# Eight masked identities of 128 rows in place of 16 rows of one, for the matmul that opens a counting block

## The reference, cut to what matters

```python
loop = jnp.arange(n, dtype=edge_index.dtype)
src = jnp.concatenate([edge_index[0], loop])
dst = jnp.concatenate([edge_index[1], loop])
deg = jax.ops.segment_sum(jnp.ones_like(dst, dtype=x.dtype), dst, num_segments=n)
...
msg = h[src] * norm[:, None]
out = jax.ops.segment_sum(msg, dst, num_segments=n)
```

## Time and profile before

| what | value |
|---|---|
| median of 3 executions | 856.17 us (855.83 to 856.72) |
| the profiled execution's span, first to last instruction | 855.8 us |
| TensorE busy (matmuls) | 823.9 us, 96% |
| VectorE busy | 672.8 us, 79% |
| ScalarE busy | 270.3 us, 32% |
| GpSimd busy | 58.5 us, 7% |
| mean granted TensorE clock | 0.997 |

### The profile page before, as it was taken

The page is one execution under the profiler, slowest core; times in us unless marked ns, Lnnn a source line. Parts: engine busy times, 40 slices in busy tenths (PEclk is TensorE's granted clock), DMA queues, the critical chain, the costliest instruction groups (busy, mean ns, idle before and its releaser), DMA issues.

```text
span 855.8 us, 13745 instructions
## 1 busy us (share of the span) xinstructions
PE 823.9 (96%) x5022; PEld 531.2 (62%) x5022; DVE 672.8 (79%) x1181; ACT 270.3 (32%) x510; POOL 58.5 (7%) x77
## 2 busy tenths in 40 slices
PE   5999999999899999999999998999999999999995
PEld 4566665566554444445888887886666666655553
DVE  6998885787675757999988889969973196996686
ACT  3443445300111110104554536644311007770000
POOL 2000002001103000000000000002101000000111
PEclk9999999999999999999999999999999999999998
DMA  8000003123131225217111313123212242212231
GB/s 304 4 2 2 1 2 126 43 68 152 62 155 68 74 74 223 87 70 231 54 48 51 103 32 114 58 81 120 91 62 93 75 154 74 93 56 74 74 111 70
DMA packets 24588, 73.55 MB, mean 86 GB/s; under 512 B 2756, under 2 KB 3756, under 8 KB 24398
## 3 DMA queue, kind: packets, MB, share of 16 engines
q1 hardware_dynamic: 23262, 67.61, 23.0%
q0 software_dynamic: 1264, 5.11, 1.8%
HBM read 52.40 MB, written 20.31 MB: 85 GB/s over the span
## 4 chain that ended last, share of the span: by engine, by line
PE 81%; DVE 10%; issue 3%; DMA 2%; ACT 1%; DVEq 1%; SPq 0%; POOL 0%; POOLq 0%
PE psum L949 18%; PE psum L976 18%; PE psum L1057 11%; PE psum L743 9%; PE psum L864 8%; DVE arena L1449 6%; PE psum L755 6%; PE psum L807 4%; PE psum L800 1%; PE psum L964 1%; PE psum L990 1%; DMA arena<-as_scratch 1%; PE psum L901 1%; PE psum L716 1%; DMA arena<-uv_scratch 1%
## 5 line engine op out<-in xcount | busy, mean ns | idle before, releaser
L976 PE MATMUL psum<-arena 128*128 128x257 f32 x800 | 175.4, 381 | 3.7 <-DVE arena L1593 2.6
L1064 ACT ACTIVATE arena<-psum 128x160 f16<-128x160 f32 (+6 forms) x188 | 93.4, 527 | 257.4 <-PE psum L743 74.7
L976 PEld LDWEIGHTS psum<-arena 128*128 128x128 f32 x800 | 151.2, 190 | 27.4 <-ACT arena L1064 2.7
L743 PE MATMUL psum<-arena 128*128 128x512 f16 x720 | 159.4, 379 | 2.4 <-DVE arena L1421 2.1
L949 PE MATMUL psum<-arena 128*128 128x512 f16 x960 | 158.5, 326 | 0.2 <-ACT arena L1064 0.2
L949 PEld LDWEIGHTS psum<-arena 128*128 128x128 f16 x960 | 93.5, 97 | 62.3 <-ACT arena L1064 0.5
L743 PEld LDWEIGHTS psum<-arena 128*128 128x128 f16 x720 | 69.2, 98 | 86.5 <-issue 7.1
L1057 PE MATMUL psum<-arena 128*128 128x512 f16 (+2 forms) x600 | 98.4, 325 | 0.0
L1449 DVE CUSTOM_DVE_ANT_0 arena<-arena 128x1280 bf16<-128x1280 bf16 x50 | 71.0, 1488 | 15.4 <-DMA arena<-as_scratch 9.6
L1057 PEld LDWEIGHTS psum<-arena 128*128 128x128 f16 x600 | 58.3, 97 | 39.8
L1167 ACT ACTIVATE arena<-arena 128x640 f32<-128x640 f32 x80 | 64.6, 836 | 51.5 <-DVE arena L1578 51.3
(11 more groups left out here) (169 smaller groups left out, 710.2 us busy)
## 6 DMA issues: line engine op xcount, KB each, us to landing
arena<-in_L_gnn_W_dram SPq DMA_DIRECT2D x22, 384.0 KB, 3.4
r_scratch<-arena SPq DMA_DIRECT2D x10, 512.0 KB, 2.6
arena<-uv_scratch SPq DMA_DIRECT2D x16, 320.0 KB, 4.4
arena<-r_scratch SPq DMA_DIRECT2D x10, 512.0 KB, 3.8
x_scratch<-arena SPq DMA_DIRECT2D x10, 384.0 KB, 4.5
arena<-x_scratch SPq DMA_DIRECT2D x10, 384.0 KB, 3.5
r_scratch<-arena SPq DMA_DIRECT2D x10, 384.0 KB, 2.6
arena<-r_scratch SPq DMA_DIRECT2D x10, 384.0 KB, 3.9
```

Of the source, the lines that this page charges most:

```text
L743: ins = pe.matmul(o[:, a:b], part[:, k, ds(t * P, P)], w[:, k, a:b], start=(not begun and k == 0 and n == 0 and m == 0), stop=(k == kn - 1 ...
L976: last = pe.matmul(p_att[:, ATT_BANKS[ch][j], 0:HID + 1], pf[n % PSLOTS][:, j * P:(j + 1) * P], xl[ch % H][:, k, 0:HID + 1], start=(k == 0 ...
L1064: act.activation(out_, in_, ACT.Copy, scale=scale).then_inc(signal, 1)
```

## The change

The opening matmul of a block reads all 128 partitions of both operands in place of the first 16. For that, GpSimd makes `own_rows`, eight matrices of 128 x 128 side by side: number j is the identity with all but its rows 16 j to 16 j + 15 zero. The moving operand is a window of `ident_w`, which is widened from 304 to 416 columns. The product is the same 128 x 160 block as before. `ident_w` and `own_rows` move to bytes 185 K and 183 K of each partition, memory that is used for something else later, so `ident_h` gets a tile of its own. TensorE waits once, ahead of block 0, for four new GpSimd instructions (semaphore `own_ok`).

```diff
-        SELF = (T - 1) * WD
-        ident_w = small([SELF + T * WD], f16)
-        ident_h = ident_w[:, SELF:SELF + P]
-        assert SELF >= P - WD and T * WD >= P
+        ident_h = small([P], f16)
...
+        SELF, STEP = (T - 1) * WD, P + WD
+        own_rows = at(183 * KB, [SUBS * P], f16)
+        ident_w = at(185 * KB, [SELF + P - WD + T * WD], f16)
+        assert 4 * D * (T - 1) == 27 * KB and SUBS * P + SELF + P - WD + T * WD <= 2 * D
...
-            for m, shift, width in ((ident, 0, P), (ident_w, SELF, SELF + T * WD)):
+            for m, shift, width in ((ident, 0, P), (ident_w, SELF, SELF + P - WD + T * WD)):
                 pool.affine_select(out=m, in_=m, compare_op=ALU.not_equal, fill=1.0, base=shift,
                                    pattern=[[-1, width]], channel_multiplier=1).then_inc(S["ident_ok"], 1)
             pool.wait_ge(S["ident_ok"], 4)
-            pool.tensor_scalar(less_h, ident_h, -1.0, None, ALU.mult).then_inc(S["iotas"], 1)
+            pool.tensor_scalar(less_h, ident_w[:, SELF:SELF + P], -1.0, None, ALU.mult).then_inc(S["iotas"], 1)
...
             pool.memset(half, -0.5).then_inc(S["half_ok"], 1)
+            pool.memset(own_rows, 0.0).then_inc(S["own_ok"], 1)
+            pool.tensor_copy(ident_h, ident_w[:, SELF:SELF + P]).then_inc(S["own_ok"], 1)
+            pool.wait_ge(S["own_ok"], 2)
+            pool.tensor_copy(own_rows[:, 0:(SUBS - 1) * STEP].rearrange("p (j c) -> p j c", j=SUBS - 1)[:, :, 0:WD],
+                             ident_h[:, 0:P - WD].rearrange("p (j c) -> p j c", j=SUBS - 1)).then_inc(S["own_ok"], 1)
+            pool.tensor_copy(own_rows[:, (SUBS - 1) * STEP:], ident_h[:, P - WD:]).then_inc(S["own_ok"], 1)
...
                 t, row = b // SUBS, b % SUBS * WD
-                own = pe.matmul(o, ident_w[0:WD, SELF - row:SELF - row + P], ident_w[0:WD, SELF - t * WD:SELF - t * WD + T * WD],
-                                start=True, stop=True)
+                own = pe.matmul(o, own_rows[:, b % SUBS * P:(b % SUBS + 1) * P],
+                                ident_w[:, SELF + row - t * WD:SELF + row - t * WD + T * WD], start=True, stop=True)
...
             pe.wait_ge(S["ranges_i"], 1)
             pe.wait_ge(S["iotas"], IOTAS)
+            pe.wait_ge(S["own_ok"], 4)
```

## The result

| | before | after |
|---|---|---|
| median of 4 executions each | 856.11 us (855.83 to 856.72) | 846.2 us (844.18 to 846.28) |
| ratio | | 0.9872 (0.9861 to 0.9884) |
| span of the profiled execution | 855.8 us | 842.3 us |
| time of that execution | (not on record) | 844.18 us |
| last opening matmul starts | 138.8 us | 127.7 us |

The account below looks back on a forecast made before the run. VectorE was taken to set the pace up to 38.8 us, TensorE from there to 138.8. Terms 12.9 - 0.2 + 0.1 - 0.3 gave 12.5 us, so span 843.3 and time 843.7 us; range 842.0 to 847.5, its own narrower one 842.5 to 845.5.

Parts of the forecast that it names:

- The price of an opening matmul: Counting stage, blocks 14 to 79: about 0.10 us lost on each side, 0.195 us gained per block, 12.9 us in all.
- Whenever the number of rows changes: Claimed cause of the gaps around opening matmuls: TensorE's array empties at any change of row count, 0.10 us either side.
- The half-gain rival: Only the side behind the opening matmul gains, its load waiting for blk_free: 6.6 us, 849.6 us; chance 0.07.
- The blocks behind the degrees: Eight counting-stage blocks following one-column matmuls: side ahead gives 0.07 us, not 0.10, so 0.2 us less in all.
- Block 19: Counting stage: TensorE would be ready at 46.31 us but the block's keys come at 46.64, so 0.3 us less gain.
- VectorE becomes the bound: Rival: in the counting stage VectorE can't follow TensorE; loss of 1 to 5 us, 845 to 849 us; chance 0.08.
- 12.9 - 0.2 - 0.3: Counting-stage terms: 66 blocks' gain of 12.9 us, less 0.2 for blocks behind the degrees and 0.3 for block 19.
- GpSimd's setup: Before block 0: four added instructions end at 10.7 us, 14.3 at double price, some 8 us of cover; no cost.
- The forecast's own sign of being wrong: At block 0, listed among what the profile would show if wrong: TensorE's first opening matmul later than 18.6 us.
- The wider mask: Setup: identity mask of 416 columns for 304 lengthens two instructions by 0.13 us each; taken as nothing, at most 0.3.
- Span and time: End of the sum: span 843.3 us turned into time 843.7, as the runs' median was 0.4 above the profiled span.
- All after 140 us shifts with TensorE: Everything behind the counting stage follows no other clock and shifts with TensorE, by one amount.

Follow-up runs that it names:

- e3: Changed kernel with the opening matmul reading 16 to 128 rows, stepped by block of a tile; 850.64 us, one execution, against 855.82 for the kernel before.
- e4: e2 with the 20 bias matmuls of the second layer's residual also reading 128 rows, zeros below row 2; 844.27 us.
- e2: Changed kernel with the four table instructions on ScalarE in place of GpSimd; 843.95 us, and 844.4 us when run again.
- e5: Changed kernel with the four table instructions still on GpSimd but waiting until VectorE's seven int16 passes are done; 844.79 us.
- a1_after_again: The changed kernel run again unaltered; 846.12 us against 857.15 for the kernel before on that chip, ratio 0.9869.

## Why the prediction was right or wrong

- **The price of an opening matmul** was right: 0.17 became 0.07 and 1.07 became 0.97, and by exact starts most blocks gain 0.20 to 0.21. The cause was right in kind: e3 and e4 show that it is the count of rows, not the code around it. "Whenever the number of rows changes" was too wide: 80, 96 and 112 rows lose nothing beside 128. The half-gain rival (the load with its wait isn't pulled ahead) falls: that load starts 0.07 ahead.
- **The blocks behind the degrees** were mis-sized: 0.165 each in my sum, 0.12 measured, since the side ahead gave 0.05 for 0.07 and the side behind 0.07 for 0.10. Eight of them, one of which gained only 0.03: 0.4 us. Blocks 25 and 41, which come right behind such a block with no product between, were counted at 0.195 and gained nothing (L807 of block 25 waits until 56.04 us; what for, the trace doesn't say): 0.4 more. The other blocks' 0.01 above the price gives that back.
- **Block 19** cost 0.26 for 0.3. The rest of the rival "VectorE becomes the bound" did not come: from block 13's first loop matmul to block 79's opening matmul there were 138.83 - 38.96 = 99.87 us by the trace of before, and are 127.7 - 39.90 = 87.8: 12.1 gained, and 12.4 by my terms (12.9 - 0.2 - 0.3).
- **GpSimd's setup was the step that failed.** I costed it at nothing because own_ok had 8 us of cover, and it had: the four instructions ended at 8.9 us, where 10.7 was forecast. I asked only who waits for their end, and not whom their running holds up. VectorE's first L1291 was held for 1.1 us, on the very chain that I had named as setting the pace up to block 13. Measured: block 13 0.94 us late, and 0.9 to 1.0 us given back at block 79 by e2 and e5. The forecast's own sign of being wrong, a first opening matmul later than 18.6 us, came with it (19.2).
- **The wider mask**, taken at nothing, cost some 0.1 us in all the new kernels: its memset lasts 0.43 us for 0.34, VectorE's passes start at 6.74 for 6.61, and with ScalarE's tables block 13 starts at 38.97, where 38.86 was forecast. No run left the wider mask out, so this cause is argued from the times and not shown.
- **Span and time.** The step from 843.3 of span to 843.7 of time was wrong: time is span + 1.8 to 2.2. And the execution profiled before was one in which the VectorE chain set the start of the attention layer, 2.3 us later than TensorE's would have. With both put right, and 11.1 us of gain: 855.8 - 11.1 + 1.8 to 2.2 = 846.5 to 846.9 when that chain is as late as it was, and 2.3 us less, 844.2 to 844.6, when TensorE's comes last. The measured 844.18 to 846.4 lie within these ends.
- "All after 140 us shifts with TensorE" did not hold: at the attention layer two chains are level within 2.3 us. Block 79 opens 11.1 us earlier and the attention layer starts 13.5 us earlier in the profile of after, 11.7 in that of a1_after_again.
- **The range** held by luck. It was made wider than 845.5 for the case that VectorE becomes the bound in the counting stage, and that did not come; the median went beyond 845.5 by the setup and by the step from span to time, neither of which the range was made for.

What stays open is why the trip through as_scratch takes 8.3 us in one execution and 10 in another. The version with the tables on ScalarE has the lower median both times, 843.95 and 844.4 against 846.12 and 845.32 of the changed kernel beside it; the intervals overlap, and the profiles show 0.9 to 1.0 us of it.

## What to carry to other kernels

In this kernel a matmul of 64 rows or fewer between matmuls of 128 costs 0.2 us more than one padded with zeros to 80 or more (0.12 behind matmuls of one column), where TensorE sets the pace; look at the distance to its neighbours, not at its duration. When setup work is added to GpSimd, ask not only who waits for its result but which VectorE instruction runs beside it, on whichever chain sets the pace then. And know which chain the profiled execution took before turning its span into a time.

## What the runs showed of the hardware

- TensorE loses 0.10 us ahead of a matmul of 64 rows or fewer and 0.10 behind it when its neighbours have 128: shown with 2, 16, 32, 48 and 64 rows. With 80, 96 and 112 rows nothing is lost.
- A VectorE pass over int16 of 0.32 us lasted 1.46, until 0.10 us behind the end of a GpSimd memset; one with a PSUM operand kept its 0.61 us beside the same memset.
- Behind matmuls of one column, a matmul of 128 rows and 160 columns and its follower stand 0.10 us apart, not 0.07.
- A trip of the same rows through memory and back took 8.3 to 10.05 us, issue to first use, in ten profiled executions. With up to 8.95 us the attention layer started 256.0 to 256.6 us behind block 79's opening, with 9.5 and more 257.1 to 258.4.
